# Reordering the head rows of the exact attention's query and key, freeing score banks in three late sections, and moving a small multiply from GpSimd to VectorE

## The chip, the cores and the metric

The kernel runs on one core of a Trainium2 chip. The metric is the device time of one execution in microseconds (us), lower is better. The core has TensorE (PE), VectorE (DVE), ScalarE (ACT), GpSimd (POOL) and SyncE (SP, which here only issues transfers), and 16 DMA engines.

## The reference

Two transformer layers run over x of 8 batches x 512 tokens x 256 features with 16 heads of 16 features, float32.

```
# layer 0
x = attn_fq(ln1(x), ln1(x)) + x      # s=0: q, k, v and softmax rounded to 8-bit steps
x = attn_fq(ln2(x), ctx) + x         # s=1: the same, keys and values from ctx
x = (a * gelu(g)) @ ff_w2 + ff_b2 + x ; a, g = split(ln3(x) @ ff_w1 + ff_b1)   # s=2
# layer 1
x = ln1(x + attn(x, x, x, causal))   # s=3: exact attention, biases on q, k, v
x = ln2(x + attn(x, ctx, ctx))       # s=4: exact attention
x = ln3(x + moe(x))                  # 8 experts of 256x1024x256, best 2 for each token
```

## The kernel before

**Stages and order.** The program first runs everything up to the expert layer, in `transformer`, and then the experts, in `experts`, in 71 blocks of 128 rows that each load their expert's weights (2 MB a block). In `transformer` the work of a batch is cut into steps named by kind, batch B, stage s and number n: for instance `S`, `M`, `nb`, `E`, `R`, `Q`, `T`, `ev`, `AV` of a quantised attention (s=0, 1) and `A`, `am`, `ms`, `MT`, `mt`, `B`, `E2`, `AV2`, `n1`, `n2`, `n3` of an exact one (s=3, 4). `program_steps` gives each step and what stands before it. `program_order` walks through them with a table of durations (`TIMES`, two numbers each: how long the engine is taken, and until the result is there), a table of offsets to each step's urgency (`URGENT`) and a tolerance (`AHEAD`), and so writes one fixed order for every engine. Each engine then issues its steps in this order, in order, each with its waits on semaphores. Where the order sees a gap of 400 ns or more on PE, it puts in filler products (`W`, line 1616), which nothing reads.

Quantised and exact sections alternate: while one works through its units, the neighbour's units go in between. Behind the last quantised section (batch 7, s=1) exact sections follow each other: (6,4), (7,3), (7,4).

**A quantised unit** (512 of them: 8 batches x 2 x 32) takes two heads' scores of 128 queries (`S`, two banks of PSUM), their maximum on DVE (`M`, line 1444), the bias of the exponential (`nb`, 1447), two exponentials on ACT that also sum the row (`E`, 1583), the reciprocal of the sums on DVE (`R`, 1450), on POOL first `rstep` = reciprocal x inverse step (1210) and then two roundings of 128x512 (`Q`, 1214), transposes on PE (`T`, 1726), and a copy on DVE (`ev`, 1456).

**An exact section** needs float32 scores from bf16 products. Query and key are therefore split on POOL into three bf16 parts (`spk`, `spq`, lines 1222 to 1228), 128 rows (8 heads) at a time: halves n=0 and n=1. SP writes the three parts to DRAM (`psk`, `psq`, line 1092: 384 KB), and reads them back as stacks of 6 x 16 rows for each head (`pkk`, `pkq`, line 1105): six transfers for the key and six for the query, 128 KB each, with a destination of 16 partitions. Row 16h+r of the half belongs to head h, so that each partition of a stack gathers 8 runs of 1 KB:

```
Q_PART = [0, 0, 1, 0, 2, 1]
K_PART = [0, 1, 0, 2, 0, 1]
sp.dma_start(dst[DH * c:DH * (c + 1), 8 * n:8 * n + 8, :],
             scratch["qk".index(which), part, n * P:(n + 1) * P, :].rearrange("(h r) n -> r h n", r=DH))
```

The products `A` (line 1749) of a half wait for both stacks of this half. Their maxima (`am`, 1464) are turned and laid under the query as more rows (`ms` on POOL, `MT` 1758, `mt` 1591); `B` (1771) then gives the shifted scores transposed, `E2` (1602, 1604) the exponentials and `AV2` (1788) the sums. A section has 64 pairs of (head, key tile): the first 48 go as 24 steps `B` of two key tiles each, in banks (2,3) and (4,5) in turn. The last 16 (those of the last 4 heads) go one by one, all in bank 5, as 16 steps, in every section, so that the other banks are free for the section that follows. The key stack of the second half may be overwritten only behind the last `B` of the exact section before.

Of the kernel before, what the change touches and what calls it, by code (L numbers as in the profile page):

```python
# [15 lines left out]
P = 128  # L16
# [39 lines left out]
Q_PART = [0, 0, 1, 0, 2, 1]  # L56
K_PART = [0, 1, 0, 2, 0, 1]
# [18 lines left out]
def place_taken(B):  # L76
# [4 lines left out]
RING = 6  # L81
BIAS_ROW = {0: "a1_bo", 1: "a2_bo", 2: "ff_b2"}
# [30 lines left out]
AHEAD = 49  # L113
TIMES = {
# [6 lines left out]
    "pkk": (2700, 4900), "pkq": (2700, 4900), "psk": (500, 2700), "psq": (500, 2700), "qi": (330, 417), "rL": (1703, 1923),  # L121
# [47 lines left out]
    ("pkk", 3): (62808,), ("pkk", 4): (183907,), ("pkq", 3): (-166118,), ("pkq", 4): (31837,), ("psk", 3): (18890,),  # L169
    ("psk", 4): (-214331,), ("psq", 3): (175825,), ("psq", 4): (28044,), ("q", 0): (-12327,), ("q", 1): (-9249,),  # L170
# [4 lines left out]
    ("spk", 3): (4677,), ("spk", 4): (-39167,), ("spq", 3): (311675,), ("spq", 4): (8974,), ("st", 0): (-41642,),  # L175
# [17 lines left out]
def b_place(n):  # L193

    if n < PAIRED:
        return n // 8, n // 4 % 2, n % 4, (0, 1)
    return NG - 1, (n - PAIRED) // 8, n % 8 // 2, (n % 2,)


def b_banks(n):  # L200

    if n >= PAIRED:
        return (5,)
# [2236 lines left out]
```

## Time and profile before

| | |
|---|---|
| median of 3 runs | 3247.3 us (3240.66 to 3247.51) |
| the profiled execution's own time | 3252.41 us |
| its span, first to last instruction | 3250.6 us |
| PE / DVE / ACT / POOL busy over the span | 90% / 67% / 60% / 49% |
| granted TensorE clock, mean | 0.96 |
| DMA | 344 MB, 106 GB/s in the mean; 325 to 333 GB/s from 2700 to 3100 us |

PE's busy share holds the filler products, and the ends of matmuls are modelled. Busy times of a line count overlapping records in full, so that the start of the next instruction says better than a record's length what an instruction costs its engine. An idle time in brackets stands ahead of the instruction, with what released it; "issue" is a wait for which the profile shows no releaser.

### The profile page before, as it was taken

Reading aid. Unit: us, or ns where it says so; the run is one execution under the profiler, and the core shown is the slowest. Engines: PE = TensorE matmul, PEld = TensorE weight load, DVE = VectorE, ACT = ScalarE, POOL = GpSimd, SP = SyncE. Lnnn points to the kernel's source line nnn. Section 1 sums busy time; section 2 is a strip of 40 time slices with the busy share of each in tenths; the row PEclk is TensorE's granted clock in tenths of the full one; section 3 lists DMA queues with packets and bytes.
Section 4 is the critical chain, followed back from the end, with each engine's and each line's share of the span. In section 5 each row is a group of like instructions: output and inputs, shape, how many; then the busy total and the mean of one; then the engine's idle time right before and its main releaser. Section 6 shows DMA issues by size and latency. Waiting matters only on the chain. (4 is left out here: it accounts for less than half of the span.)

```text
span 3250.6 us, 58872 instructions
## 1 busy us (share of the span) xinstructions
PE 2931.8 (90%) x19207; PEld 1704.7 (52%) x19207; DVE 2182.8 (67%) x4597; ACT 1957.1 (60%) x4182; POOL 1586.8 (49%) x2770
## 2 busy tenths in 40 slices
PE   6999999999999999999999999988898889999991
PEld 3445443544354445435443544454444349999991
DVE  4796797789788877978797788778755632111115
ACT  3666667676757675867668576757454244444442
POOL 4675483667367545836583566365722512111115
PEclk9999999999999999999999999998998899999995
DMA  3002231333042214212330323040532329999995
GB/s 97 14 14 62 66 78 30 77 63 71 27 92 59 59 33 101 55 48 60 72 79 30 84 47 66 24 92 30 153 101 52 95 90 328 328 326 328 325 324 157
DMA packets 296133, 344.22 MB, mean 106 GB/s; under 512 B 33550, under 2 KB 273294, under 8 KB 295616
## 3 DMA queue, kind: packets, MB, share of 16 engines
q1 hardware_dynamic: 287664, 323.35, 36.3%
q0 software_dynamic: 6480, 17.58, 1.6%
q8 instruction: 140, 2.29, 0.3%
q14 instruction: 121, 0.99, 0.1%
q10 hardware_dynamic: 1728, 0.01, 0.0%
HBM read 291.50 MB, written 51.23 MB: 105 GB/s over the span
## 5 line engine op out<-in xcount | busy, mean ns | idle before, releaser
L1583 ACT ACTIVATE quant<-ps,nbias,sc 128x512 f32<-128x512 f32 x1024 | 791.1, 779 | 268.4 <-DVE nbias L1447 225.4
L1214 POOL TENSOR_SCALAR quant<-quant,rstep 128x512 f16<-128x512 f32 x1024 | 713.5, 697 | 152.3 <-PE ps L1726 59.5
L1464 DVE TENSOR_REDUCE m<-ps 128x1 f32<-128x512 f32 (+3 forms) x1024 | 561.1, 583 | 275.3 <-PE ps L1749 142.0
L1444 DVE TENSOR_REDUCE nmax<-ps 128x2 f32<-128x1024 f32 x512 | 619.8, 1214 | 73.7 <-PE ps L1718 69.6
L1749 PE MATMUL ps<-kst,qst 96*128 96x512 bf16 (+3 forms) x1024 | 323.5, 355 | 72.5 <-issue 42.7
L1456 DVE TENSOR_SCALAR big<-ps 128x1024 bf16<-128x1024 f16 x512 | 348.5, 681 | 52.4 <-PE ps L1726 48.1
L2147 ACT ACTIVATE hT<-moe_ps,expert_b 128x128 f32<-128x128 f32 x568 | 207.2, 368 | 269.0 <-PE moe_ps L2061 232.6
L1602 ACT ACTIVATE big<-ps 128x512 f32<-128x512 f32 (+3 forms) x640 | 273.5, 479 | 118.8 <-PE ps L1774 68.5
L1726 PE MATMUL ps<-id,quant 128*128 128x128 f16 x4096 | 322.3, 223 | 20.2 <-DVE big L1456 14.7
L1726 PEld LDWEIGHTS ps<-id,quant 128*128 128x128 f16 x4096 | 253.2, 99 | 160.2 <-issue 84.1
L1771 PE MATMUL ps<-qst,kst 108*128 108x512 bf16 (+3 forms) x1024 | 298.4, 350 | 38.3 <-ACT big L1602 22.6
L2342 DVE COPY words<-plain_rows 128x3 uint32 x71 | 12.0, 169 | 416.7 <-PE moe_ps L2113 416.7
L2003 POOL DMA_INDIRECT rows_out<-yb,words x71 | 69.2, 975 | 436.2 <-DVE yb L2349 433.5
L1696 PE MATMUL ps<-xT,wring 128*128 128x512 f32 x512 | 262.6, 621 | 4.4 <-ACT qst L1591 3.7
L1616 PE MATMUL ps<-idb 128*128 128x512 bf16 x873 | 240.2, 390 | 27.0 <-DVE sc L1262 19.8
L1749 PEld LDWEIGHTS ps<-kst,qst 96*128 96x128 bf16 x1024 | 98.7, 100 | 299.1 <-DVE m L1464 187.7
L1718 PE MATMUL ps<-quant 32*128 32x512 bf16 x1024 | 199.0, 394 | 47.3 <-ACT quant L1583 35.0
L1788 PE MATMUL ps<-big,v_f 128*32 128x512 f32 (+3 forms) x2048 | 225.7, 525 | 3.6 <-ACT big L1602 2.6
L1210 POOL TENSOR_TENSOR rstep<-rinv,inv_step 128x2 f32<-128x2 f32 x512 | 101.5, 198 | 249.1 <-DVE rinv L1450 230.4
L1234 POOL CAST mparts<-m 128x16 bf16<-128x16 f32 x64 | 13.8, 215 | 423.7 <-DVE m L1464 423.7
L1591 ACT ACTIVATE qst<-ps 12x1024 bf16<-12x1024 bf16 x128 | 124.2, 1010 | 157.4 <-PE ps L1758 156.8
L1771 PEld LDWEIGHTS ps<-qst,kst 108*128 108x128 bf16 x1024 | 97.3, 99 | 226.2 <-issue 159.8
(292 smaller groups left out, 5336.6 us busy)
## 6 DMA issues: line engine op xcount, KB each, us to landing
e_w<-in_L_xattn_e_w_dram SPq DMA_DIRECT2D x70, 1024.0 KB, 7.5
quant<-in_L_xattn_e_w_dram SPq DMA_DIRECT2D x36, 1024.0 KB, 7.3
uT<-in_L_xattn_e_w_dram SPq DMA_DIRECT2D x36, 1024.0 KB, 6.7
wring<-in_L_xattn_ff_w_dram SPq DMA_DIRECT2D x96, 256.0 KB, 2.9
parts<-parts_sb SPq DMA_DIRECT2D x64, 384.0 KB, 2.4
kst<-parts SPq DMA_DIRECT2D x192, 128.0 KB, 4.3
qst<-parts SPq DMA_DIRECT2D x192, 128.0 KB, 5.1
plain_rows<-rows_in SPq DMA_DIRECT2D x71, 140.0 KB, 2.6
```

The costliest lines, as they stand in the source:

```text
L1214: nc.gpsimd.tensor_scalar(pq[:, u % 2, h, :], probs[:, u % 2, h, :], rstep[:, u % 2, h:h + 1], HALF_ROUND, ALU.mult, ALU.add).then_inc(SIG ...
L1444: nc.vector.tensor_reduce(nmax[:, n % 2, :], ps[:, a:a + 2, :], AX.X, ALU.max, negate=True).then_inc(SIG["M"], 1)
L1456: nc.vector.tensor_scalar(probs_t[:, g % 2, 2 * p:2 * p + 2, :, t * P:(t + 1) * P], PT, -HALF_ROUND, WMAX, ALU.add, ALU.min).then_inc(SIG[ ...
L1464: nc.vector.tensor_reduce(m32[:, g % 2, t, h:h + 1], bank(("A", B, s, n))[:, 0:width], AX.X, ALU.max, negate=True).then_inc(SIG["am"], 1)
L1583: nc.scalar.activation(probs[:, u % 2, h, :], ps[:, BANKS[("S", B, s, u)][h], :], ACT.Exp, bias=nbias[:, u % 2, h:h + 1], scale=sc[:, s:s ...
L1602: last = nc.scalar.activation(ex[:, half, h, j, i0:N], ps[:, from_, i0:N], ACT.Exp, scale=SCALE)
L1616: nc.tensor.matmul(ps[:, BANKS[e][0], :], idb[:, :], idb[:, :].unsqueeze(1).broadcast_to([P, NT, P]), start=True, stop=True)
L1696: last = nc.tensor.matmul(bank(e), wt[:, k, (f % 2) * P:(f % 2 + 1) * P], xT[:, k, :], start=(k == 0), stop=(k == KT - 1))
L1726: last = nc.tensor.transpose(PT[:, h, j, :], pq[:, n % 2, h, j * P:(j + 1) * P], id16[:, :])
L1749: last = nc.tensor.matmul(bank(e)[:, 0:width], qst[0:PAIR_ROWS, head, t * P:(t + 1) * P], kst[0:PAIR_ROWS, head, 0:width], start=True, sto ...
L1771: last = nc.tensor.matmul(dst[:, i0:N], kst[0:rows_, head, jt * P:(jt + 1) * P], qst[0:rows_, head, i0:N], start=True, stop=not causal(s))
L1788: last = nc.tensor.matmul(OUTX[SLOT * h:SLOT * (h + 1), i0:N], v_f32[:, jt, SLOT * head:SLOT * (head + 1)], ex[:, half, h, j, i0:N], start ...
```

## The change

Four things change.

1. **The copies.** Rows of a half are ordered r*8+h in place of h*16+r, so that the 8 heads of a feature lie next to each other: in DRAM a stack's partition is then one run of 8 KB. For this the columns of the four weights (query and key, s=3 and 4) are permuted once, at the start: SP loads them (4 x 256 KB) into `uT`, ACT copies them turned in one instruction of 128x2048 (behind `dT` of batch 0, s=1), and ACT's queue writes them to DRAM (`by_row`, 1 MB). The weight pieces of k and q are from then on read from there. The order of the parts becomes [0,0,0,1,1,2] and [0,1,2,0,1,0]. The key is still written as three parts, and read in three transfers of 48, 32 and 16 partitions. The query is written as six parts (768 KB in three transfers, repeating the source), and read in one transfer of 96 partitions (768 KB).
2. **The banks.** In the three sections that no quantised one follows (`WHOLE`: (6,4), (7,3), (7,4)), the last 16 pairs go as 8 steps of two tiles in both pairs of banks, as the others.
3. **The step.** `rstep` is computed by DVE, as a step `RS` of its own behind `R`, and no longer by POOL ahead of `Q`.
4. **The order.** `TIMES` of the changed steps, all of `URGENT`, and `AHEAD` (49 to 84) are new, so the order of all engines is another.

```diff
-Q_PART = [0, 0, 1, 0, 2, 1]
-K_PART = [0, 1, 0, 2, 0, 1]
+Q_PART = [0, 0, 0, 1, 1, 2]
+K_PART = [0, 1, 2, 0, 1, 0]
+Q_RUNS = [(0, 3), (3, 2), (5, 1)]
+K_RUNS = [(0, 3), (3, 2), (5, 1)]
...
-AHEAD = 49
+AHEAD = 84
...
-    "pkk": (2700, 4900), "pkq": (2700, 4900), "psk": (500, 2700), "psq": (500, 2700)
+    "pkk": (1300, 5500), "pkq": (500, 4500), "psk": (500, 2700), "psq": (1300, 4500)
-    ("Q", 0): (1074, 985), ("Q", 1): (772, 692)
+    ("Q", 0): (772, 692), ("Q", 1): (772, 692), "RS": (73, 155)
...
+WHOLE = {(B, s) for B in range(NBATCH) for s in (3, 4) if before_exact(B, s)}
-def b_place(n):
-    if n < PAIRED:
+def b_place(B, s, n):
+    if n < PAIRED or (B, s) in WHOLE:
         return n // 8, n // 4 % 2, n % 4, (0, 1)
     return NG - 1, (n - PAIRED) // 8, n % 8 // 2, (n % 2,)
-def b_banks(n):
-    if n >= PAIRED:
+def b_banks(B, s, n):
+    if n >= PAIRED and (B, s) not in WHOLE:
         return (5,)
     return (2, 3) if n % 2 == 0 else (4, 5)
...
+            for i, (kind, s) in enumerate(BY_ROW):
+                sp.dma_start(as_given[:, i, :, :], w[WEIGHT[s] + kind].rearrange("(k p) n -> p k n", p=P)).then_inc(s_given, 16)
             load_wo(3, "sa_wo")
...
+                    if which == "k":
+                        sp.dma_start(scratch[1, n, 0:3].rearrange("c p n -> p c n"), parts[:, slot % 2, :, :])
+                    else:
+                        for part, (c, times) in enumerate(Q_RUNS):
+                            sp.dma_start(scratch[0, n, c:c + times].rearrange("c p n -> p c n"),
+                                         parts[:, slot % 2, part:part + 1, :].broadcast_to([P, times, N]))
...
-                    for c, part in enumerate(order):
-                        sp.dma_start(dst[DH * c:DH * (c + 1), 8 * n:8 * n + 8, :],
-                                     scratch["qk".index(which), part, n * P:(n + 1) * P, :].rearrange("(h r) n -> r h n", r=DH))\
+                    for c, parts_here in K_RUNS if which == "k" else ((0, len(Q_PART)),):
+                        sp.dma_start(dst[DH * c:DH * (c + parts_here), HEADS * n:HEADS * (n + 1), :].rearrange("p h n -> p (h n)"),
+                                     scratch["qk".index(which), n, 0:parts_here].rearrange("c (r h) n -> (c r) (h n)", r=DH))\
...
                     if h == 0:
-                        after(pool, "R", B, s, u)
-                        after_ordinal(pool, "Q", NO[e] - 3)
-                        nc.gpsimd.tensor_tensor(rstep[:, u % 2, :], rinv[:, u % 2, :],
-                                                inv_step[:, 4 * s + 3:4 * s + 4].broadcast_to([P, 2]), ALU.mult).then_inc(s_steps, 1)
-                        pool.wait_ge(s_steps, i + 1)
+                        after(pool, "RS", B, s, u)
...
+                if kind == "RS":
+                    after(dve, "R", B, s, n)
+                    nc.vector.tensor_tensor(rstep[:, n % 2, :], rinv[:, n % 2, :], inv_step[:, 4 * s + 3:4 * s + 4].broadcast_to([P, 2]),
+                                            ALU.mult).then_inc(SIG["RS"], 1)
...
+                if (kind, B, s, n) == ("dT", 0, 1, 1):
+                    act.wait_ge(s_given, 16 * len(BY_ROW))
+                    nc.scalar.activation(row_major..., as_given..., ACT.Identity).then_inc(s_turned_cols, 1)
+                    act.wait_ge(s_turned_cols, 1)
+                    act.dma_start(by_row.rearrange("i k p n -> p (i k) n"), row_major...).then_inc(s_by_row, 16)
```

## Rows read from the trace of the kernel before

**Rows 1.** Windows of 100 us: busy time of each engine, clock, DMA share, GB/s.

```profile
core 0: us, PE busy (x) PEld busy (x) DVE busy (x) ACT busy (x) POOL busy (x), PEclk, DMA share, GB/s
900.00:1000.00 100.00, 91.95 (x699) 52.47 (x698) 78.96 (x169) 64.05 (x144) 58.56 (x106) 0.98 0.39 93
1000.00:1100.00 100.00, 90.21 (x634) 47.12 (x635) 92.19 (x182) 70.01 (x164) 80.49 (x142) 0.98 0.30 67
1100.00:1200.00 100.00, 95.36 (x518) 40.26 (x519) 74.51 (x130) 74.65 (x125) 34.07 (x70) 0.98 0.09 27
...
2500.00:2600.00 100.00, 85.50 (x451) 40.50 (x450) 61.77 (x190) 33.50 (x63) 60.11 (x83) 0.83 0.36 88
...
2900.00:3000.00 100.00, 100.00 (x690) 94.22 (x689) 18.24 (x56) 43.87 (x123) 12.64 (x13) 1.00 0.98 325
```

**Rows 2.** Timeline of PE, 2590 to 2668 us: start, length, what, idle ahead.

```profile
2659.48 0.41 PE L2051 MATMUL moe_ps<-id,plain_rows 128*128 128x128 f32 x2 [2.41 <-DVE credit L2206]
```

**Rows 3.** Groups by line and shape on PE, 60 to 2160 us.

```profile
L1749 PE MATMUL ps<-kst,qst 96*128 96x128 bf16 x100 | 20.5, 242 | 36.1 <-issue 32.3 <-DMA qst<-parts 2.1 <-DVE m L1464 1.5
```

**Rows 4.** Timeline of PE: the first `A` of halves of exact sections.

```profile
941.58 0.22 PE L1749 MATMUL ps<-kst,qst 96*128 96x128 bf16 x1 [4.35 <-issue]
...
1245.41 0.27 PE L1749 MATMUL ps<-kst,qst 96*128 96x128 bf16 x1 [5.92 <-issue]
...
2437.66 0.26 PE L1749 MATMUL ps<-kst,qst 96*128 96x128 bf16 x1 [4.50 <-DMA qst<-parts]
...
2475.60 0.27 PE L1749 MATMUL ps<-kst,qst 96*128 96x128 bf16 x1 [4.81 <-issue]
```

**Rows 5.** Timeline of SP's queue, 925 to 950 us.

```profile
924.55 2.68 SPq L1092 DMA_DIRECT2D parts<-parts_sb  x2
...
929.07 2.79 SPq L1105 DMA_DIRECT2D kst<-parts  x6
...
932.43 2.78 SPq L1105 DMA_DIRECT2D qst<-parts  x6
```

**Rows 6.** Windows of 2 us while these copies run.

```profile
936.00:938.00 2.00, 1.23 (x8) 0.40 (x5) 2.00 (x4) 1.40 (x4) 1.85 (x3) 1.00 1.14 184
```

**Rows 7.** Timeline of ACT in the last two exact sections.

```profile
2509.05 0.60 ACT L1602 ACTIVATE big<-ps 128x512 f32<-128x512 f32 x1 [0.45 <-PE ps L1788]
...
2530.51 0.28 ACT L1602 ACTIVATE big<-ps 128x128 f32<-128x128 f32 x1 [0.46 <-PE ps L1774]
...
2602.18 3.77 ACT L1604 ACTIVATE big<-ps 128x1024 f32<-128x1024 f32 x4 [0.47 <-PE ps L1771]
...
2629.01 0.60 ACT L1602 ACTIVATE big<-ps 128x512 f32<-128x512 f32 x1
...
2648.20 0.60 ACT L1602 ACTIVATE big<-ps 128x512 f32<-128x512 f32 x1 [0.56 <-PE ps L1771]
```

**Rows 8.** Timeline of DVE, 1010 to 1030 us.

```profile
1011.02 0.16 DVE L1450 RECIPROCAL rinv<-rsum 128x2 f32<-128x2 f32 x1
1011.10 1.20 DVE L1444 TENSOR_REDUCE nmax<-ps 128x2 f32<-128x1024 f32 x1
...
1021.53 1.09 DVE L1447 TENSOR_SCALAR nbias<-nmax,sc 128x2 f32<-128x2 f32 x1
```

**Rows 9.** Timeline of POOL, 1010 to 1024 us.

```profile
1011.26 0.20 POOL L1210 TENSOR_TENSOR rstep<-rinv,inv_step 128x2 f32<-128x2 f32 x1 [0.55 <-DVE rinv L1450]
1011.56 1.48 POOL L1214 TENSOR_SCALAR quant<-quant,rstep 128x512 f16<-128x512 f32 x2
...
1021.45 1.15 POOL L1228 TENSOR_TENSOR parts_sb<-kf,parts_sb 128x512 bf16<-128x512 f32 x1
```

**Rows 10.** Groups on DVE, 1000 to 1100 us.

```profile
L1447 DVE TENSOR_SCALAR nbias<-nmax,sc 128x2 f32<-128x2 f32 x30 | 11.9, 397 | 0.2
```

**Rows 11.** The page's costliest groups, whole span.

```profile
L1210 POOL TENSOR_TENSOR rstep<-rinv,inv_step 128x2 f32<-128x2 f32 x512 | 101.5, 198 | 249.1 <-DVE rinv L1450 230.4
```

**Rows 12.** Timeline at the start, SP's queue and DVE.

```profile
41.20 1.53 SPq L1025 DMA_DIRECT2D X<-in_x_dram  x3
...
45.33 0.75 DVE L1276 BATCH_NORM_STATS2 bn<-X 128x6 f32<-128x256 f32 x2 [23.73 <-DMA X<-in_x_dram]
```

More of the change, by code:

```diff
@@ L81 @@
 RING = 6
+BY_ROW = [(kind, s) for s in (3, 4) for kind in "kq"]
 BIAS_ROW = {0: "a1_bo", 1: "a2_bo", 2: "ff_b2"}
@@ L190, in s_pair, with before_exact, shifted, last_b @@
     return u % 2
-def b_place(n):
-    if n < PAIRED:
+def before_exact(B, s):
+    line = sorted((section_of(z, b), b, z) for b in range(NBATCH) for z in (0, 1, 3, 4))
+    after = line[line.index((section_of(s, B), B, s)) + 1:]
+    return not after or after[0][2] >= 3
+def shifted(B, s):
+    return UNITS if (B, s) in WHOLE else SHIFTED
+def b_place(B, s, n):
+    if n < PAIRED or (B, s) in WHOLE:
         return n // 8, n // 4 % 2, n % 4, (0, 1)
     return NG - 1, (n - PAIRED) // 8, n % 8 // 2, (n % 2,)
-def b_banks(n):
-    if n >= PAIRED:
+def b_banks(B, s, n):
+    if n >= PAIRED and (B, s) not in WHOLE:
         return (5,)
     return (2, 3) if n % 2 == 0 else (4, 5)
-def last_b(g, p):
-    return 8 * g + 4 * p + 3 if g < NG - 1 else PAIRED + 8 * p + 7
-def ex_half(g, p):
-    return p if g < NG - 1 else 1
-FILLS_HALF = [[n for n in range(SHIFTED) if n == 0 or b_place(n)[:2] != b_place(n - 1)[:2] if ex_half(*b_place(n)[:2]) == half]
-              for half in range(2)]
+def last_b(B, s, g, p):
+    return 8 * g + 4 * p + 3 if g < NG - 1 or (B, s) in WHOLE else PAIRED + 8 * p + 7
+def ex_half(B, s, g, p):
+    return p if g < NG - 1 or (B, s) in WHOLE else 1
+def fills_half(B, s, half):
+    return [n for n in range(shifted(B, s)) if n == 0 or b_place(B, s, n)[:2] != b_place(B, s, n - 1)[:2]
+            if ex_half(B, s, *b_place(B, s, n)[:2]) == half]
 def times(kind, B, s, n):
@@ L397, in project @@
                 step("ps" + which, B, s, m, ("sp" + which, B, s, 3 * m + 2), stage and ("pk" + which, *stage, m))
-                step("pk" + which, B, s, m, ("ps" + which, B, s, m), stage and ("B", *stage, (15, SHIFTED - 1)[m]))
+                step("pk" + which, B, s, m, ("ps" + which, B, s, m), stage and ("B", *stage, (15, shifted(*stage) - 1)[m]))
         if s < 2:
@@ L447, in quantised @@
             step("AV", B, s, n, ("ev", B, s, 8 * g + 7), ("vi", B, s, 2), n and ("AV", B, s, n - 1),
-                 n == 8 and ("do", B, s, 0), n == 0 and tail("E2", SHIFTED - 1))
+                 n == 8 and ("do", B, s, 0), n == 0 and tail("E2", ahead and shifted(*ahead) - 1))
         for m in range(KT):
@@ L465, in exact @@
                 step("mt", B, s, 2 * g + i, ("MT", B, s, g))
-            for n in range(SHIFTED):
-                if b_place(n)[0] != g:
+            for n in range(shifted(B, s)):
+                if b_place(B, s, n)[0] != g:
                     continue
-                p, h = b_place(n)[1:3]
-                mine = [v for v in range(n) if set(b_banks(v)) & set(b_banks(n))]
-                step("B", B, s, n, ("mt", B, s, 2 * g + h // 2), ("E2", B, s, mine[-1]) if mine else tail("do", 1) or same("E2", SHIFTED - 1))
-                half = ex_half(g, p)
-                at = FILLS_HALF[half].index(n) if n in FILLS_HALF[half] else None
-                before_g, before_p = b_place(FILLS_HALF[half][at - 1])[:2] if at else (0, 0)
+                p, h = b_place(B, s, n)[1:3]
+                mine = [v for v in range(n) if set(b_banks(B, s, v)) & set(b_banks(B, s, n))]
+                step("B", B, s, n, ("mt", B, s, 2 * g + h // 2), ("E2", B, s, mine[-1]) if mine else tail("do", 1) or same("E2", ahead and shifted(*ahead) - 1))
+                half = ex_half(B, s, g, p)
+                fills = fills_half(B, s, half)
+                at = fills.index(n) if n in fills else None
+                before_g, before_p = b_place(B, s, fills[at - 1])[:2] if at else (0, 0)
                 step("E2", B, s, n, ("B", B, s, n), at and ("AV2", B, s, NT * before_g + 2 * before_p + 1),
@@ L478, in exact @@
                 n = NT * g + j
-                step("AV2", B, s, n, ("E2", B, s, last_b(g, j // 2)), ("dV", B, s, 1), n and ("AV2", B, s, n - 1),
+                step("AV2", B, s, n, ("E2", B, s, last_b(B, s, g, j // 2)), ("dV", B, s, 1), n and ("AV2", B, s, n - 1),
                      j == 0 and g and ("n1", B, s, g - 1))
@@ L792, in transformer @@
     QF_BEFORE = sequence(lambda kind, B, s, n: kind == "dq" and n == 0)
-    HALF_BEFORE = [sequence(lambda kind, B, s, n: kind == "ev" and n % 16 == 8 * half or kind == "E2" and n in FILLS_HALF[half])
+    HALF_BEFORE = [sequence(lambda kind, B, s, n: kind == "ev" and n % 16 == 8 * half or kind == "E2" and n in fills_half(B, s, half))
                    for half in range(2)]
@@ L796, in transformer, with parts_sent @@
     PARTS_NO = {e: n for n, e in enumerate(PARTS_SEQ)}
+    def parts_sent(n):
+        return 16 * sum(1 if e[0] == "dk" else len(Q_RUNS) for e in PARTS_SEQ[n % 2:n + 1:2])
+    STACK_LOADS = {"k": 16 * len(K_RUNS), "q": 16}
     Q_STAGES = [(B, s) for kind, B, s, n in ORDER if kind == "S" and n == 0]
@@ L1003, in load_piece @@
                     after(sp, *PIECES[i - RING][1])
-                if kind in "kqv":
+                if (kind, s) in BY_ROW:
+                    if (kind, s) not in told:
+                        told.add((kind, s))
+                        sp.wait_ge(s_by_row, 16)
+                    src = by_row[BY_ROW.index((kind, s))].rearrange("k p n -> p k n")
+                elif kind in "kqv":
                     src = w[WEIGHT[s] + kind].rearrange("(k p) n -> p k n", p=P)
@@ L1090, in _ @@
                     if stage:
-                        sp.wait_ge(s_stack[(which, n)], 96 * (X_STAGES.index(stage) + 1))
-                    sp.dma_start(scratch["qk".index(which)][:, n * P:(n + 1) * P, :].rearrange("c p n -> p c n"), parts[:, slot % 2, :, :])\
-                        .then_inc(s_parts[slot % 2], 16)
+                        sp.wait_ge(s_stack[(which, n)], STACK_LOADS[which] * (X_STAGES.index(stage) + 1))
+                    if which == "k":
+                        sp.dma_start(scratch[1, n, 0:3].rearrange("c p n -> p c n"), parts[:, slot % 2, :, :]).then_inc(s_parts[slot % 2], 16)
+                    else:
+                        for part, (c, times) in enumerate(Q_RUNS):
+                            sp.dma_start(scratch[0, n, c:c + times].rearrange("c p n -> p c n"),
+                                         parts[:, slot % 2, part:part + 1, :].broadcast_to([P, times, N])).then_inc(s_parts[slot % 2], 16)
                 if kind in ("pkk", "pkq"):
@@ L1096, in _ @@
                     slot = PARTS_NO[("d" + which, B, s, n)]
[L1097 removed]
+                    sp.wait_ge(s_parts[slot % 2], parts_sent(slot))
                     stage = before(X_STAGES, B, s)
                     if stage:
[L1100 removed]
+                        after(sp, "B", *stage, (15, shifted(*stage) - 1)[n])
                     else:
                         sp.wait_ge(s_ones, 16 * NG)
[L1103 to L1106 removed]
+                    for c, parts_here in K_RUNS if which == "k" else ((0, len(Q_PART)),):
+                        dst = kst if which == "k" else qst
+                        sp.dma_start(dst[DH * c:DH * (c + parts_here), HEADS * n:HEADS * (n + 1), :].rearrange("p h n -> p (h n)"),
+                                     scratch["qk".index(which), n, 0:parts_here].rearrange("c (r h) n -> (c r) (h n)", r=DH))\
                             .then_inc(s_stack[(which, n)], 16)
@@ L1593, in _ @@
                 if kind == "E2":
-                    g, p, h, js = b_place(n)
-                    half, banks = ex_half(g, p), BANKS[("B", B, s, n)]
+                    g, p, h, js = b_place(B, s, n)
+                    half, banks = ex_half(B, s, g, p), BANKS[("B", B, s, n)]
                     after(act, "B", B, s, n)
-                    if n in FILLS_HALF[half]:
+                    if n in fills_half(B, s, half):
                         half_free(act, half, e)
@@ L1744, in _ @@
                         for which in "kq":
[L1745 removed]
+                            pe.wait_ge(s_stack[(which, n // 32)], STACK_LOADS[which] * (X_STAGES.index((B, s)) + 1))
                     bank_free(pe, e)
@@ L1778, in _ @@
                     p, j, i0 = jt // 2, jt % 2, lo(s, jt)
-                    half = ex_half(g, p)
+                    half = ex_half(B, s, g, p)
                     if jt == 0:
@@ L2409, in build @@
         s_expert = [es.enter_context(nc.semaphore(f"expert_loaded{i}")) for i in range(WSLOTS)]
-        transformer(nc, parts, args["x"], args["ctx_1024"], args, mid, rows_in, kept, s_sc, s_zeroed, s_eb, s_block, s_expert)
+        transformer(nc, parts, by_row, args["x"], args["ctx_1024"], args, mid, rows_in, kept, s_sc, s_zeroed, s_eb, s_block, s_expert)
         experts(nc, rows_in, rows_out, args, out, kept, s_sc, s_zeroed, s_eb, s_block, s_expert)
```

51 lines of the change are left out of this document (32 added, 19 removed), and 96 rows, old and new, of tables (MEANS, ON, TIMES, URGENT).

## The prediction

> **What bounds the kernel now.** I read the windows first. Behind 2659 us the experts run [rows 2]: DMA share 0.98 at 325 GB/s with PE full [rows 1]. Nothing of the change stands there, so 3250.6 - 2659.5 = 591 us stay, and every microsecond that `transformer` ends earlier moves the end by one. Up to about 2150 us the program repeats itself: the first `A` of s=3 comes at 941.58 and at 1245.41 us [rows 4], so a batch takes 303.8 us. In three windows of such a period [rows 1] PE is busy 90 to 95%, fillers included, DVE 79, 92 and 75%, POOL 59, 80 and 34%. No engine is full all the time: PE carries most, and from 1000 to 1100 us DVE is the bound. Then I looked for waits that stop all engines. There is one in each period: the first `A` of s=3 waits for its operands' copies. The row of this shape has 36.1 us of idle time ahead of it, of which 32.3 + 2.1 = 34.4 us are "issue" and the query's DMA [rows 3]: seven sections, 4.9 us each. Two more of 4.50 and 4.81 us stand in (7,3) [rows 4]. Behind 2200 us the work thins out: from 2500 to 2600 us DVE has 62%, ACT 34% and POOL 60% [rows 1], so there chains of single steps set the time.
>
> **The copies.** In the section of batch 2 the parts are written from 924.55 us, the key's six loads are issued from 929.07, the query's six from 932.43 to 935.21 [rows 5], and `A` starts at 941.58 [rows 4]: 12.5 us from the first load, for 12 x 128 KB = 1.57 MB. Meanwhile the DMA engines are full (share above 1) but move only 184 GB/s [rows 6], against 325 in the expert stage [rows 1]. So the transfers are slow, not merely many. The change issues them in 4 transfers. What rate they reach the trace doesn't show; it lies between 184 GB/s (nothing gained) and 325 (the expert weights, 128 partitions). I take the middle, 250, as the query now goes to 96 partitions and the key to 48, 32 and 16. Then 1.57 MB take 6.3 us, and with some 2 us up to the first landing (12.5 less 8.5 us, which 1.57 MB take at 184 GB/s, is 4; half of it is the drawn-out issue) that is 8.3 in place of 12.5: -4.2 us. Against this the query's parts are now 0.39 MB more to write, at 250 GB/s 1.6 us, in the same DMA engines and ahead of the loads. The order allows the query's way 4.5 + 4.5 us, before 2.7 + 4.9, so PE is given about 1.4 us more of other work ahead of `A`; I count 0.9 of it. -4.2 + 1.6 - 0.9 = -3.5 us for each of seven sections: -24 us. In (7,3) I take -6 of the 9.3 us. Together **-30 us**. Bounds: at 184 GB/s 10.5 us in place of 12.5, and 2.1 more for the writes: 0. At best all 34.4 + 9.3 = 44 us.
>
> The Trainium skill speaks against the run length as the cause: *DMA: Bandwidth & Descriptors*, section Specifications, asks for at least 512 B for line rate, which 1 KB runs already have; by this alone the term would be 0, which is a rival below. Its page *SBUF — State Buffer*, section "Door 1: The DMA port swizzle", has the rate go by the ports that a transfer's partitions reach, 27.2 GB/s each: partitions 0 to 47 reach 8 ports, an estimate of 218 GB/s from this page, and 96 partitions reach all. The trace agrees with the direction (184 into 16 partitions, 325 into 128), and the sum by this page of the Trainium skill would be about the same.
>
> SP's queue also loses 8 of 12 issues of some 0.46 us (2.79/6) and gains 2 for the query's write, each half: the weight loads queued behind come earlier. Nothing waits there at present that I can price: 0.
>
> **The banks.** At the end of (7,4) the 16 single exponentials run from 2629.01 to 2648.80 us, 19.8 us, PE and ACT taking turns on one bank. Paired ones in two pairs of banks follow each other at 3.77/4 = 0.94 us [rows 7]: 8 x 0.94 = 7.5. Nothing else runs then: -12.3 us. In (7,3) the same stretch goes from 2509.05 to 2530.79, 21.7 us [rows 7]; its causal pairs are no longer than 0.94, so at least 14.2 us go, but other work stands between, which must be done in any case: I take two thirds, -9. In (6,4) the singles are interleaved with (7,3)'s first `A`; as (7,3)'s second key stack may load only behind the last of them, I take -4 (0 to -9). Together **-25 us**, bounds -12 (only the last section) and -36.
>
> **The step.** POOL loses an instruction whose start stands 0.30 us ahead of its `Q` (1011.26, 1011.56 [rows 9]): 512 x 0.30 = 154 us of POOL's time. But POOL stood idle 230 us waiting for DVE's reciprocal ahead of it [rows 11], so it is mostly not POOL that is late. DVE gains 512 instructions. The cheapest price is 0.08 us, the distance from a reciprocal to the next instruction (1011.02 to 1011.10 [rows 8]), if another step stands between. Directly behind its reciprocal the new one must wait until this has ended (0.16 in place of 0.08). And it can be held up: `nb`, as small as it, takes 397 ns in the mean where DVE is full [rows 10], and once 1.09 us, from 1021.53 to 1022.62 [rows 8], as a POOL instruction runs from 1021.45 to 1022.60 [rows 9]: the two exclude each other. The dearest price is thus 0.08 + 0.40 = 0.48. I take 0.25. 30 of a period's 64 units fall into the window in which DVE has no room [rows 1, 10]: 8 x 30 x 0.25 = +60 us; elsewhere it is hidden in DVE's idle quarter. POOL's 0.30 us in the same 240 units would be -72 if POOL were the bound; at 80% busy [rows 1] I give it 45 of this, as `Q` starts and frees its buffers earlier. Net **+15 us**; bounds -20 and +75 (no give-back, 0.31 us).
>
> The Trainium skill names this exclusion, in *SBUF — State Buffer*, section "Who interferes with whom": a VectorE instruction with two SBUF inputs, as the new one, and a GpSimd one hold the same ports, each for its whole length. The rows above show it, with `nb`; it is the ground of the rival that ends slower.
>
> **The start.** The first units wait in DVE's queue behind the statistics of batch 1, and these for x [rows 12], whose loads SP issues at 41.20 us, behind all constants. Four more issues (about 0.5 us each) and 1 MB more in the DMA engines (3.2 us at 325 GB/s) stand ahead of them now; ACT gets an instruction of 2048 elements later. **+4 us**, 0 to +8.
>
> **The order.** All offsets are new. No row prices this; I take 0, and +-15.
>
> **Sum.** 3252.4 - 30 - 25 + 15 + 4 = 3216.4 for the profiled execution; this one stands 5.1 us above the median of the runs, so 3211 us for the median.
>
> **The rivals.**
> *All of it lands.* Copies -44, banks -36, step -20, start +4: 3247 - 96 = 3151. For it: the whole machine stands still in each of the waits, and the new order allows more for the copies. Against: two waits in series rarely go to nothing. Chance 0.15.
> *The copies are no faster.* Run length was not the limit and extra writes eat the rest: term 0 (or a little above), the other terms as above: 3241. For it: 1 KB runs reach 325 GB/s elsewhere (the second expert matrix has such rows). Against: 184 GB/s at a full share must have a cause, and the partitions change with the runs. Chance 0.10.
> *The step costs more than the rest brings (slower).* Place: DVE from 1000 to 1100 us of each period. Price 0.31 us and above x 240 = +75 and no give-back, more where `Q` now waits for a maximum of 1.20 us that was put between `R` and `RS`. With half of the copies' gain: 3247 - 15 - 25 + 75 + 4 = 3286. It decides from about 0.25 us x 240 = 60 us without give-back (3247 - 30 - 25 + 60 + 4 = 3256). For it: DVE is 92% busy there, and the blocked `nb`. Against: where POOL waits idle for the step, it can't block it. Chance 0.15.
>
> **How the numbers follow.** Likeliest, 0.60: 3211, its own range 3180 to 3238. The range 3160 to 3258 leaves out most of the best and half of the slower case. A measurement of this kernel tells differences from about 0.2%, 6.5 us. Faster: 0.60 x 0.97 + 0.15 + 0.10 x 0.45 = 0.78; within 0.2%: 0.06; slower: 0.16.
>
> **What would show it.** Copies: one load of `qst` of 768 KB in each half, more than 184 GB/s at full share, and the idle time ahead of the first `A` of s=3 down from 4.9 to some 1.5 us. Banks: 8 instructions of line 1604's kind in a row at 0.94 us at the end, experts' first product some 35 us earlier. Step: 512 multiplies on DVE of 0.2 to 0.4 us, DVE's busy time up by 100 us or more, POOL's down by 100. The period of 303.8 us shrinks by some 2: 3.5 for the copies less 2 for the step. Wrong it is if the period grows (the step), or if the waits of [rows 3] stay.

## The result, and the profile after

The changed kernel takes 3205.1 us in the median of its runs (3200.7 to 3210.7), beside 3247.4 for the kernel before (3240.7 to 3252.5) on the same chip: a ratio of 0.987, with an interval of 0.985 to 0.990. The prediction was 3211. Set side by side with five rounds more it was 3205.8, ratio 0.986 (0.985 to 0.988). The experiments below show that the sum came out right through two large errors that cancel, so that the agreement is in good part luck.

Three instants cut the profiled execution: the first scores on PE, the last reciprocal on DVE of the quantised sections, and the experts' first product. This table has them in us for the two kernels and eight of the experiments further down, read from the timelines. "Repeating part" is the time from the first instant to the second, "tail" from the second to the third, and "experts" from the third to the end. Single executions of one kernel differ by some 10 us, so differences of a few us in it mean little.

| kernel | first scores | repeating part | tail | experts | span |
|---|---|---|---|---|---|
| before | 49.94 | 2259.2 | 350.4 | 591.1 | 3250.6 |
| after | 54.29 | 2237.8 | 321.1 | 588.8 | 3202.0 |
| copies alone | 53.95 | 2240.7 | 347.3 | 590.3 | 3232.3 |
| banks alone | 50.47 | 2251.9 | 321.4 | 591.9 | 3215.7 |
| step alone | 50.38 | 2304.2 | 349.6 | 591.6 | 3295.8 |
| copies and banks | 54.15 | 2244.9 | 319.2 | 591.6 | 3209.8 |
| copies, banks, step | 54.32 | 2281.2 | 315.8 | 591.9 | 3243.2 |
| all, offsets of before | 54.62 | 2376.8 | 327.9 | 591.6 | 3351.0 |
| after, old copies | 50.87 | 2254.5 | 320.9 | 589.4 | 3215.7 |
| after, step on POOL | 54.00 | 2227.1 | 321.0 | 591.6 | 3193.7 |

The timeline of PE in the changed kernel has the experts' first product 46 us earlier than that of the kernel before [rows 2]:

```profile
2613.24 0.41 PE L2113 MATMUL moe_ps<-id,plain_rows 128*128 128x128 f32 x2 [2.41 <-DVE credit L2268]
```

The group of the first `A` products, 60 to 2160 us, answers to [rows 3]; the idle time of 36.1 us has become 6.8:

```profile
L1811 PE MATMUL ps<-kst,qst 96*128 96x128 bf16 x104 | 19.8, 226 | 6.8 <-issue 3.6 <-DMA kst<-parts 1.7 <-DVE m L1517 1.5
```

The windows of one period, beside [rows 1]. DVE, which had 79% in the first of the three, has 89% now; in the second it has 94%:

```profile
900.00:1000.00 100.00, 93.63 (x751) 53.17 (x750) 89.37 (x204) 70.37 (x158) 62.49 (x98) 1.00 0.36 101
1000.00:1100.00 100.00, 90.30 (x615) 46.50 (x613) 94.11 (x205) 65.61 (x157) 72.76 (x106) 0.95 0.28 75
1100.00:1200.00 100.00, 97.71 (x499) 42.07 (x500) 74.68 (x140) 75.20 (x120) 29.09 (x53) 0.98 0.09 27
```

The timeline of SP's queue, beside [rows 5]: the key's read is one group of three issues, the query's one issue.

```profile
926.20 1.45 SPq L1145 DMA_DIRECT2D parts<-parts_sb  x3
...
929.81 1.59 SPq L1158 DMA_DIRECT2D qst<-parts  x1
933.58 1.25 SPq L1158 DMA_DIRECT2D kst<-parts  x3
```

The timeline of ACT at the end of (7,4), beside [rows 7]: the last four heads are now eight exponentials of two tiles, from 2594.55 us, 0.94 us apart while they run in a row.

```profile
2594.55 5.61 ACT L1666 ACTIVATE big<-ps 128x1024 f32<-128x1024 f32 x6
2600.62 1.94 ACT L1666 ACTIVATE big<-ps 128x1024 f32<-128x1024 f32 x2 [0.47 <-PE ps L1833]
```

And the groups of the two smallest DVE instructions from 1000 to 1100 us, beside [rows 10]:

```profile
L1496 DVE TENSOR_SCALAR nbias<-nmax,sc 128x2 f32<-128x2 f32 x29 | 12.2, 419 | 0.2
L1502 DVE TENSOR_TENSOR rstep<-rinv,inv_step 128x2 f32<-128x2 f32 x30 | 7.5, 250 | 0.4
```

### The profile page after: what moved, and what is told of

The parts are those of the page before. It is cut to its first block and busy times, and to the rows that moved or that the text cites. A ratio compares the mean times of both kernels' runs of the same rounds, so it can differ in the third digit from the quotient of the medians.

```text
span 3202.0 us, 57992 instructions
## 1 busy us (share of the span) xinstructions
PE 2905.9 (91%) x19128; PEld 1688.7 (53%) x19128; DVE 2257.2 (70%) x5109; ACT 1960.0 (61%) x4167; POOL 1497.5 (47%) x2258
## 5 line engine op out<-in xcount | busy, mean ns | idle before, releaser
L1263 POOL TENSOR_SCALAR quant<-quant,rstep 128x512 f16<-128x512 f32 x1024 | 714.2, 697 | 470.9 <-DVE rstep L1502 219.8
L1664 ACT ACTIVATE big<-ps 128x256 f32<-128x256 f32 (+1 forms) x608 | 251.1, 467 | 92.0 <-PE ps L1836 52.6
L1833 PE MATMUL ps<-qst,kst 108*128 108x512 bf16 (+3 forms) x1024 | 287.9, 345 | 16.3 <-ACT big L1664 7.5
L1758 PE MATMUL ps<-xT,wring 128*128 128x512 f32 x512 | 259.2, 615 | 1.4 <-ACT uT L1627 0.9
L1678 PE MATMUL ps<-idb 128*128 128x512 bf16 x794 | 213.9, 384 | 23.5 <-DVE sc L1311 20.0
L1666 ACT ACTIVATE big<-ps 128x1024 f32<-128x1024 f32 x208 | 200.8, 1027 | 24.1 <-PE ps L1833 17.6
L1645 ACT ACTIVATION_READ_ACCUMULATOR quant<-ps,nbias,sc 128x1 f32 x1024 | 206.4, 202 | 0.0
L1735 PE MATMUL ps<-xT,wring 128*128 128x512 f32 x384 | 200.2, 623 | 5.5 <-ACT parts_sb L1614 2.0
```

Source lines behind the costliest of these rows:

```text
L1263: nc.gpsimd.tensor_scalar(pq[:, u % 2, h, :], probs[:, u % 2, h, :], rstep[:, u % 2, h:h + 1], HALF_ROUND, ALU.mult, ALU.add).then_inc(SIG ...
L1645: nc.scalar.activation(probs[:, u % 2, h, :], ps[:, BANKS[("S", B, s, u)][h], :], ACT.Exp, bias=nbias[:, u % 2, h:h + 1], scale=sc[:, s:s ...
L1664: last = nc.scalar.activation(ex[:, half, h, j, i0:N], ps[:, from_, i0:N], ACT.Exp, scale=SCALE)
L1758: last = nc.tensor.matmul(bank(e), wt[:, k, (f % 2) * P:(f % 2 + 1) * P], xT[:, k, :], start=(k == 0), stop=(k == KT - 1))
L1833: last = nc.tensor.matmul(dst[:, i0:N], kst[0:rows_, head, jt * P:(jt + 1) * P], qst[0:rows_, head, i0:N], start=True, stop=not causal(s))
```

## The experiments

The sum of the prediction has five terms, and a total can't tell them apart. So the first three runs ask for one edit alone, in the order of the kernel before, and the fourth for all edits without the new offsets; the next four ask the same inside the changed order; the last four ask whether the terms add up, and what makes a copy slow. Ratios are to the kernel before, run on the same chip between them.

| kernel | median, us | ratio to before | interval |
|---|---|---|---|
| copies alone | 3233.6 | 0.994 | 0.992 to 0.996 |
| step alone | 3296.2 | 1.013 | 1.011 to 1.016 |
| banks alone | 3223.8 | 0.991 | 0.989 to 0.993 |
| all, offsets of before | 3350.5 | 1.030 | 1.028 to 1.032 |
| after, again | 3205.8 | 0.986 | 0.985 to 0.988 |
| after, old copies | 3219.1 | 0.991 | 0.989 to 0.992 |
| after, step on POOL | 3197.5 | 0.985 | 0.983 to 0.986 |
| after, x earlier | 3203.6 | 0.986 | 0.985 to 0.988 |
| copies and banks | 3203.7 | 0.985 | 0.983 to 0.987 |
| copies, banks, step | 3253.6 | 1.001 | 0.999 to 1.002 |
| 8 KB runs, 16 partitions | 3235.4 | 0.995 | 0.993 to 0.997 |
| 1 KB runs, 96 partitions | 3205.8 | 0.986 | 0.984 to 0.988 |

The kernel before had medians of 3251.9 (first four), 3249.5 (next four) and 3251.6 us (the other four).

### The copies alone

The changed kernel's copies and weight permutation; banks, place of the step, durations, offsets and tolerance of before. PE, DVE and POOL issue the same instructions in the same order as before. The cut is against the changed kernel:

```
-WHOLE = {(B, s) for B in range(NBATCH) for s in (3, 4) if before_exact(B, s)}
+WHOLE = set()
-            step("RS", B, s, u, ("R", B, s, u))
-AHEAD = 84
+AHEAD = 49      # and TIMES, URGENT of the kernel before
```

> The new copies and the permuted weights alone; the order of PE, DVE and POOL, the banks and the place of the step stay as in the kernel before. My theory: most of the 34 + 9 us of idle time ahead of the first A goes and the start costs 4: 25 to 38 us under the kernel before, the wait ahead of the first A at 1 to 2 us a section. Rival, the new order did the work by covering the copies: then the wait stays near 4 us a section, and the kernel is within 8 us of the kernel before.

18 us faster (18.8 by the ratio), short of the expected 25 to 38. The group of the first `A`, 60 to 2160 us:

```profile
L1809 PE MATMUL ps<-kst,qst 96*128 96x128 bf16 x103 | 20.6, 236 | 24.4 <-issue 22.6 <-DVE m L1515 1.5 <-ACT quant L1643 0.2
```

Two thirds of the wait stay in the order of before: 24.4 us, of which 22.6 are "issue", over seven sections 3.2 each. Windows of 2 us while both stacks load say why; the columns are those of [rows 1]:

```profile
928.00:930.00 2.00, 2.00 (x27) 0.77 (x25) 2.00 (x5) 2.00 (x5) 1.35 (x4) 1.00 1.08 209
930.00:932.00 2.00, 2.00 (x16) 1.09 (x12) 1.59 (x4) 1.68 (x5) 1.83 (x3) 1.00 0.88 184
932.00:934.00 2.00, 2.00 (x13) 0.81 (x12) 1.24 (x3) 2.00 (x6) 1.84 (x4) 1.00 1.14 266
934.00:936.00 2.00, 0.19 (x1) 0.00 (x0) 1.10 (x3) 1.21 (x4) 1.83 (x3) 1.00 0.96 243
```

The key's three transfers come first here (issued from 926.02 us), and the core moves 184 to 209 GB/s while they run; with the query's, issued at 928.74, it moves 243 to 266. The mean of the four windows is 225, not 250, and 11.1 us pass from the first load's issue to `A` at 937.11, in place of 12.5. A window counts everything that the core moves: SP issues weight loads of 256 KB at 925.57, 928.25 and 932.43 as well, and in the kernel before, at 928.61, 931.90 and 935.47. So neither the 225 here nor the 184 of [rows 6] is the rate of the stacks alone.

### The step alone

The kernel before with the small multiply behind the reciprocal on DVE, and GpSimd waiting for it:

```
                     nc.vector.reciprocal(rinv[...], rsum[...]).then_inc(SIG["R"], 1)
+                    dve.wait_ge(SIG["R"], NO[e] + 1)
+                    nc.vector.tensor_tensor(rstep[...], rinv[...], inv_step..., ALU.mult).then_inc(s_steps, 1)
```

> Only the small multiply goes to VectorE, directly behind its reciprocal; order, copies and banks as before. My forecast's term: 15 us over the kernel before, bounds -20 and +75. If GpSimd's relief is worth as much as VectorE's load, within 6 us; if VectorE's full window pays 0.25 us for each of 240 without anything given back, 60 us slower.

43 us slower by the ratio (1.3%), where the term was 15, and the whole of it is in the repeating part (2259.2 to 2304.2, 45.0 us). Groups on DVE, 1000 to 1100 us:

```profile
L1443 DVE TENSOR_SCALAR nbias<-nmax,sc 128x2 f32<-128x2 f32 x30 | 10.5, 352 | 0.2
L1448 DVE TENSOR_TENSOR rstep<-rinv,inv_step 128x2 f32<-128x2 f32 x29 | 8.5, 293 | 1.0
```

In this window 8.5 us come in and 1.4 leave `nb` (11.9 in [rows 10]): 7.1 us, of which 8 periods would be 57. My load on DVE, 60, was thus about right, and its place too: unit by unit, the reciprocals of this kernel fall behind those of the kernel before by 7.2 us from 920.67 to 1062.44 us (times of the kernel before), and by 1.1 from there to 1222.94. The 45 that I let GpSimd give back is what is missing: 57 less the 45 measured leaves it 12 at most. GpSimd waited 230.4 us for DVE in the kernel before [rows 11]. With 101.5 us of its own work gone it waits 328.7, so nearly all that it was relieved of turned into waiting. The page of this kernel:

```profile
L1210 POOL TENSOR_SCALAR quant<-quant,rstep 128x512 f16<-128x512 f32 x1024 | 714.3, 698 | 537.7 <-DVE rstep L1448 328.7
```

### The banks alone

`WHOLE` as in the changed kernel, all else as before.

> Only the three late sections in both pairs of banks, planned with the durations, offsets and tolerance of the kernel before. My theory: 25 us under the kernel before (12 in (7,4), 9 in (7,3), 4 in (6,4)). Rival, only the last section gains and the others' other work fills the time: 12 us under it.

28 us faster (29.3 by the ratio), a little more than the 25 of the forecast. It is in the tail, which shrinks from 350.4 to 321.4 us; the changed kernel's tail is 321.1. The profiled execution, 6 us under its median, is also 7 us shorter in the repeating part, where this edit has nothing of its own. All of that lies at its very end, where its granted clock from 2150 to 2300 us is 0.98 and that of the kernel before 0.89. The rival, that only the last section gains, is out.

### All edits, offsets of before

```
-AHEAD = 84
+AHEAD = 49      # and URGENT of the kernel before; TIMES stay as changed
```

> All edits, but the offsets and the tolerance of the kernel before, so that the order is made from these. If the new order has no share in the result, as in my sum (term 0), it is within 10 us of the changed kernel, that is some 40 us under the kernel before. If the new order is where the gain is, it lies between the kernel before and 20 us under it, or above.

99 us slower than the kernel before, 145 slower than the changed one: far outside the first expectation, and beyond what the second, with its "or above", had in mind. The filler products show where it arises. They stand where the order, when it is written, sees a gap of 400 ns or more on PE, so their number tells how full the order was planned, before anything runs. The changed kernel's group on PE over the whole span, then this kernel's:

```profile
L1678 PE MATMUL ps<-idb 128*128 128x512 bf16 x794 | 213.9, 384 | 23.5 <-DVE sc L1311 20.0
```

```profile
L1676 PE MATMUL ps<-idb 128*128 128x512 bf16 x1070 | 291.4, 389 | 26.1 <-DVE sc L1309 20.7 <-ACT xT L1558 4.8 <-ACT rT L1575 0.3
```

276 fillers more, 78 us of PE: the order itself was written with larger gaps, before any of it ran. The kernel before has 873 fillers. Three things differ from the run "copies, banks, step" below, which has the offsets of before too and yet takes only 3253.6 us: the step is planned as one of its own, the table of before has no offset for it, so that it counts as 0, and the durations are the changed ones. Which of the three opens the gaps was not tried.

### The changed kernel again, with old copies, with the step on GpSimd

All three in the changed order. The second has the old transfers, the old order of the parts and no permutation; the third this:

```
+                        nc.gpsimd.tensor_tensor(rstep[...], rinv[...], inv_step..., ALU.mult).then_inc(s_steps, 1)
+                        pool.wait_ge(s_steps, i + 1)
...
-                if kind == "RS":
-                    after(dve, "R", B, s, n)
-                    nc.vector.tensor_tensor(rstep[...], rinv[...], inv_step..., ALU.mult).then_inc(SIG["RS"], 1)
```

> The changed kernel itself, beside the next ones: 42 us under the kernel before.

> The changed kernel with the copies of before (twelve transfers of 1 KB runs, no permuted weights), in the changed order. My theory: 20 to 35 us slower than the changed kernel, with 4 to 5 us ahead of the first A of a section again. Rival, the order covers the copies whatever their speed: within 6 us of the changed kernel.

> The changed kernel with the small multiply on GpSimd again, in the changed order. By my term of +15 for the step this is 15 us faster than the changed kernel. Rival, the step on VectorE is worth something because GpSimd's part is on the path to the rounded probabilities: then it is 5 to 30 us slower.

The first repeats its time. With the old copies it is 13 us slower: between the two theories. The group of the first `A` in the kernel with old copies, 60 to 2160 us:

```profile
L1791 PE MATMUL ps<-kst,qst 96*128 96x128 bf16 x100 | 19.5, 229 | 18.9 <-DMA kst<-parts 13.0 <-issue 4.4 <-DVE m L1506 1.5
```

So the idle time ahead of the first `A` is 36.1 us with neither, 24.4 with the new copies, 18.9 with the new order, and 6.8 with both: each takes its share, 12 us and 17 us, whether the other is there or not. I had put nearly all of it down to the copies. (The kernels in the new order have the new banks and the step on DVE as well. These don't make the difference: with all three edits in the old order the idle time is 23.8 us.)

With the step on GpSimd the changed kernel is 8 us faster by the medians and 6 by the ratios, the intervals just overlapping, where my term said 15. If DVE's step still costs something here, it is a small part of what it costs in the order of before. GpSimd waits 120.7 us for DVE's reciprocal in this kernel, and 219.8 for its step in the changed one: here too the relief turns into waiting.

### x earlier

```
-            for i, (kind, s) in enumerate(BY_ROW):            # the four weights, ahead of load_wo
...
+            load_x(1)
             load_wo(3, "sa_wo")
...
+                if kind == "LX" and B == 1:                   # now behind it
+                    for i, (kind_, s_) in enumerate(BY_ROW):
...
```

> The changed kernel with x of batch 1 loaded ahead of the output weights, and the four weights to be permuted loaded behind that. VectorE's first wait for x, which the changed kernel has 4 us later than the kernel before, comes at least 4 us earlier. If the first scores depend on it as I take it, 4 to 10 us faster than the changed kernel; if other work fills that time, the same.

No difference. The timeline of DVE has the wait for x, in the changed kernel first and then in this one:

```profile
49.34 0.75 DVE L1325 BATCH_NORM_STATS2 bn<-X 128x6 f32<-128x256 f32 x2 [27.51 <-DMA X<-in_x_dram]
```

```profile
35.28 0.75 DVE L1327 BATCH_NORM_STATS2 bn<-X 128x6 f32<-128x256 f32 x2 [13.49 <-DMA X<-in_x_dram]
```

x is there 14 us earlier and the first reciprocal stands at 49.0 in place of 59.2 us, but eight units later the lead is 3 us (75.3 and 78.3) and after 32 units 1.4 (155.1 and 156.5). By the last reciprocal nothing is left (2292.2 and 2292.1). So the start's term of +4 is 4.35 us at the first scores, and most likely nothing at the end; what takes the lead up was not looked for.

### Copies and banks, without and with the step

In the order of before; the second with DVE's multiply behind its reciprocal, as in "the step alone".

> The new copies and the new banks together, the step on GpSimd, the order from the offsets and the tolerance of the kernel before. If the two edits add up (alone they gave 18.8 and 29.3 us), 48 us under the kernel before, so that it stands beside the changed kernel and the new order has paid for the step and nothing else. Rival, the new order brings a gain of its own: then this kernel is 10 us or more slower than the changed one.

> As the kernel with new copies and banks and the old offsets, and the step on VectorE directly behind its reciprocal, so that nothing else moves. If the edits add up (the step alone cost 43 us), 5 us under the kernel before. Rival, the three edits disturb each other as they did when the order was planned from the old offsets: then it comes near 100 us above it.

The first is 48 us under the kernel before: the sum of the two alone (18.8 + 29.3), which its interval of some 6 us to either side can't tell more closely, and level with the changed kernel. The second is level with the kernel before: here the step costs 49 us by the ratios. From it to the changed kernel, which has the same three edits and differs in the order, there are 46 us, by the ratios. So the new order has paid for the step on VectorE, and for little else.

### Run length or partitions

The changed kernel's transfers into the stacks in the two mixed forms, in excerpts:

```
-                    for c, parts_here in K_RUNS if which == "k" else ((0, len(Q_PART)),):
+                    for c, parts_here in [(c, 1) for c in range(6)]:      # 8 KB runs, 16 partitions each
```

```
+                        for odd in range(2):                              # 1 KB runs, 96 / 48, 32, 16 partitions
+                            sp.dma_start(dst[DH * c:DH * (c + parts_here), HEADS * n + odd:HEADS * (n + 1):2, :],
+                                         scratch[...].rearrange("c (r h) n -> (c r) h n", r=DH)[:, odd::2, :])
```

> The changed kernel, its stacks read in runs of 8 KB as before this, but in six transfers of 16 partitions each for key and query. If the run length makes the rate, over 250 GB/s while the stacks load, and the changed kernel's time. If the number of partitions of a transfer does, near 140 GB/s, as with the old copies, and some 14 us slower.

> The changed kernel, its stacks read in runs of 1 KB, in transfers of 96 (query) and 48, 32 and 16 partitions (key), even and odd heads apart. If the run length makes the rate, near 140 GB/s while the stacks load, and some 14 us slower. If the number of partitions does, over 250 GB/s and the changed kernel's time.

Long runs into 16 partitions lose 27 us of the gain, by the ratios; short runs into many partitions lose nothing. The first `A` shows it too: 18.2 us of idle time ahead of it in the first form, as with the old copies (18.9), and 5.6 in the second, as in the changed kernel (6.8). The group of the first form:

```profile
L1811 PE MATMUL ps<-kst,qst 96*128 96x128 bf16 x100 | 19.9, 234 | 18.2 <-DMA kst<-parts 8.6 <-issue 8.1 <-DVE m L1517 1.5
```

The windows while the stacks load, in four fences: old copies in the changed order (1 KB, 16 partitions), then 8 KB and 16, then 1 KB and 96 (the second line is still the query's), then the changed kernel, 8 KB and 96.

```profile
932.00:934.00 2.00, 1.42 (x11) 0.79 (x12) 1.98 (x5) 1.85 (x5) 1.03 (x3) 1.00 1.15 144
936.00:938.00 2.00, 2.00 (x15) 1.63 (x12) 2.00 (x5) 2.00 (x6) 1.37 (x2) 1.00 1.13 139
```

```profile
940.00:942.00 2.00, 1.73 (x12) 0.56 (x10) 1.79 (x6) 1.66 (x5) 1.39 (x2) 1.00 1.06 152
942.00:944.00 2.00, 1.69 (x5) 0.77 (x6) 2.00 (x6) 1.85 (x4) 1.09 (x2) 1.00 0.95 135
```

```profile
930.00:932.00 2.00, 2.00 (x23) 0.94 (x16) 2.00 (x6) 1.06 (x3) 1.46 (x3) 1.00 0.97 315
932.00:934.00 2.00, 2.00 (x14) 0.82 (x12) 2.00 (x6) 1.55 (x5) 1.32 (x3) 1.00 1.04 282
936.00:938.00 2.00, 2.00 (x6) 0.67 (x6) 2.00 (x6) 1.57 (x5) 1.39 (x2) 1.00 1.03 171
```

```profile
930.00:932.00 2.00, 1.44 (x24) 0.78 (x24) 2.00 (x3) 1.52 (x4) 1.82 (x3) 1.00 0.89 278
932.00:934.00 2.00, 2.00 (x17) 1.00 (x14) 2.00 (x6) 1.53 (x4) 1.47 (x3) 1.00 0.92 277
936.00:938.00 2.00, 1.50 (x5) 0.76 (x6) 2.00 (x6) 1.85 (x6) 1.03 (x3) 1.00 1.04 176
```

At a DMA share near 1 in all of them: about 135 to 152 GB/s into 16 partitions for either length (the means from 930 to 940 and from 940 to 948 us are 141 and 143), 277 to 315 into 96 for either length, and 171 to 176 for the key in 48, 32 and 16 partitions, again for either length. The windows from 930 to 932 us can still hold the end of a weight load, issued at 927.86 and 928.84; those from 932 to 934, with 282 and 277, start over 3 us behind it. The 8 KB runs of the change did nothing for the rate; what helps is that the new order of rows lets one transfer reach many partitions. 8 KB with 16 partitions is also slower than the old copies in the same order, by 13 us by the ratios and 16 by the medians, where I expected them level. The order is the same in both, and so is the wait ahead of the first `A`. What differs is that it writes 0.39 MB more for each query half, and that it permutes the weights at the start (first scores at 54.23 us, with the old copies at 50.87); which of the two it is was not tried.

## Why the prediction was right, and where its steps failed

| step | predicted, us | measured, us |
|---|---|---|
| copies and start | -30 + 4 | -19 in the old order, -13 in the new |
| banks | -25 | -29 |
| step | +15 | +43 alone, +49 with copies and banks, +6 to +8 in the new order |
| order | 0 | -46 with the step on DVE, -3 to -6 with it on GpSimd (within the noise) |
| sum | -36 | -44 |

**Copies: right in direction, too large, and in part another edit's.** The step that failed is "I take the middle, 250": only the query's transfer passes that (277 to 315 in the changed order), the key's runs at 171 to 209. The baseline was off as well: 8.5 us for 1.57 MB "at 184 GB/s" took a window with weight loads in it for the stacks' own rate, and with no weight load between them the old transfers move 139 to 146 GB/s, so 1.57 MB takes them 11 us. And of the 34.4 us of wait the copies take 12; 17 more go with the new order, which was the 0.9 us a section of the forecast. Of the 18.8 us that the copies are worth, 12 are this wait; by the table of instants 3 lie in the tail, where I had -6 for (7,3), and the start costs 4 at the first scores. Where the rest lies was not located. The rule of the Trainium skill in *DMA: Bandwidth & Descriptors*, section Specifications, which I weighed against the term, is right on run length (1 KB and 8 KB give the same rate here); it does not follow that the copies gain nothing, since the partitions changed as well.

**Banks: right.** In (7,4) the end in both pairs of banks runs from 2594.55 to 2602.56 us, 8.0 us, for 7.5 predicted and 19.8 before. So 12 of the tail's 29 us are here, as predicted, and 17 are left for (7,3) and (6,4), where my two cautious shares made 13; the bound was 36.

**Step: the load right, the give-back wrong.** "I give it 45 of this" has no support in the runs: GpSimd stood idle for the reciprocal before and now stands idle for the multiply, for 328.7 us in place of 230.4 in the same order. The new order takes a good 100 us off this wait, wherever the step is. The page of the changed kernel, among its costliest groups:

```profile
L1263 POOL TENSOR_SCALAR quant<-quant,rstep 128x512 f16<-128x512 f32 x1024 | 714.2, 697 | 470.9 <-DVE rstep L1502 219.8
```

GpSimd waited for DVE, so work taken from it and put on DVE gave back next to nothing; [rows 11] said so, and I discounted it. The right term was +43, and the slower rival's condition (no give-back) was nearly met. Its price was not: the multiply takes 0.29 us in the full window and `nb` gets 0.05 shorter, about 0.25 in all, as I had it. My "dearest price" of 0.48 would have made the bound 115 and not 75; nothing came near it. With +43 in place of +15 the prediction's sum would have been -8 (its order term is 0, so it is a sum for the old order); the run with all three edits in the old order shows +2.

**Order: 0 was the step that failed most.** It is worth 46 us here, three times my bound of 15. Of these, 17 are the wait ahead of the first `A` (23.8 us with the same edits in the old order, 6.8 in the new). It doesn't add speed of its own that the runs can tell: copies and banks in the old order (0.985, 0.983 to 0.987) and the same in the new one with the step on GpSimd (0.985, 0.983 to 0.986) overlap. The medians stand 6 us apart in favour of the new, the profiled executions 16, but that of copies and banks took 8 us more than its median; whether there is a gain of some us stays open. What the new order seems to do is make room, which is read from the windows and not shown by a run of its own. DVE has 79 and 92% in the two busy windows of a period [rows 1]; the same step in the changed order fills them to 89 and 94%, with PE at 94 and 90%. The reverse shows in the run with the old offsets: fitted to another set of steps, they write an order that takes 145 us longer, and 97 us longer than the same three edits with the step tied to its reciprocal.

So the two large errors nearly cancel: the step costs 34 us more than I had (49 for 15), and the order gains 46 that I had at 0. The copies gain 7 less and the banks 4 more than I had, and in all 9 us are left. The total was within its range; the reasons were half right, and that the errors met was luck. The period shrank by 3 to 4 us (from 303.8 to 300.9 between the two instants of [rows 4], from 303.1 to 299.4 in the mean of six), not by 2.

**The best version.** The changed kernel with the step on GpSimd: 3197.5 us, 52 under the kernel before and 6 to 8 under the changed one, which is at the edge of what these runs can tell. It can't be told from copies and banks in the old order (3203.7), which needs no new offsets.

## What to carry to other kernels

When a kernel's order is planned from fitted offsets, price an edit under the old order and the new one apart: a fitted order can hide a bad edit, and offsets fitted to other steps can make good edits look ruinous. Ask of each step moved between engines which of them waits for the other; here relief of the waiting one was worth 12 us at most, of 154 that were taken off it. When copies gather small rows, arrange the data so that one transfer reaches many partitions, before thinking about longer runs.

## What the runs showed of the hardware

A small DVE instruction can be held until the GpSimd instruction beside it has ended, to within 0.01 us. The multiply takes 0.15 us in the median of its 512 times in the changed kernel, but up to 1.14. The timelines of DVE and of GpSimd in the changed kernel: the multiply that starts at 1024.17 us ends at 1025.17, as the GpSimd one that began at 1024.00 ends at 1025.16; the next, at 1026.87, ends at 1027.44, as the conversion ends at 1027.43. So the conversion, with one input, holds it as well as the two-input one does.

```profile
1024.17 1.00 DVE L1502 TENSOR_TENSOR rstep<-rinv,inv_step 128x2 f32<-128x2 f32 x1
...
1026.87 0.57 DVE L1502 TENSOR_TENSOR rstep<-rinv,inv_step 128x2 f32<-128x2 f32 x1
```

```profile
1024.00 1.16 POOL L1271 TENSOR_TENSOR kf<-kf,parts_sb 128x512 f32<-128x512 f32 x1
...
1026.82 0.61 POOL L1274 CAST parts_sb<-kf 128x512 bf16<-128x512 f32 x1
```

And the six transfers into 16 partitions each, which together reach 96 partitions and are all issued within 3 us, don't reach the rate of one transfer into 96: 135 to 152 GB/s against 277 to 315, with the DMA share near 1 in both. So a full DMA share doesn't say that the transfers are fast. The Trainium skill's *SBUF — State Buffer*, section "Door 1: The DMA port swizzle", has the rate follow the ports that are reached; the order of the two rates agrees with it if each transfer is taken alone, and the runs don't show why six at once get no further.
